# A transformer layer over 128 graphs: the MLP's first product as a 2x2 block product with seven block products

## The reference

```python
nx = _layernorm(x, ln1_g, ln1_b)
q, k, v = (nx @ W + b for Wq, Wk, Wv)           # 8 heads of 64
scores = jnp.where(adj_mask, q @ k.T / 8, NEG)
out = softmax(scores) @ v
x = x + out @ Wo + bo
nx = _layernorm(x, ln2_g, ln2_b)
return x + gelu(nx @ W1 + b1) @ W2 + b2         # W1: 512 x 2048, W2: 2048 x 512
```

## Time and profile before

| | |
|---|---|
| median of 3 runs | 2245.79 us (2245.63 to 2247.95) |
| profiled execution | 2246.27 us, span 2244.5 us |
| mean granted TensorE clock | 0.997 |
| TensorE busy | 2214.6 us, 13616 matmuls |
| VectorE busy | 1158.0 us |
| ScalarE busy | 720.1 us |
| GpSimd busy | 284.0 us |
| moved by DMA | 100.12 MB, mean 45 GB/s |

### The profile page before, as it was taken

How to read it: one execution, slowest core, us unless ns; L and a number is a source line. 1 busy time by engine, 2 the same in 40 slices (tenths; PEclk the granted TensorE clock), 3 DMA queues, 4 the chain that set the end, 5 groups by cost and what they waited for, 6 DMA issues and landing times.

```text
span 2244.5 us, 33957 instructions
## 1 busy us (share of the span) xinstructions
PE 2214.6 (99%) x13616; PEld 1827.9 (81%) x13616; DVE 1158.0 (52%) x1747; ACT 720.1 (32%) x1046; POOL 284.0 (13%) x217
## 2 busy tenths in 40 slices
PE   7999999999999989999999999999999999999999
PEld 6888888888888868888888888888888888888887
DVE  4887877777877764433434434434334334334321
ACT  4434333443333434322222222222223223223222
POOL 2121111111121124311011010010010110110100
PEclk9999999999999999999999999999999999999999
DMA  4221111211211133101101001001011011011000
GB/s 148 72 66 58 58 58 62 72 58 65 86 61 39 39 104 127 66 1 38 39 1 38 25 14 38 11 28 38 1 39 38 1 39 38 1 39 38 1 19 20
DMA packets 67363, 100.12 MB, mean 45 GB/s; under 512 B 17680, under 2 KB 21776, under 8 KB 67216
## 3 DMA queue, kind: packets, MB, share of 16 engines
q1 hardware_dynamic: 61696, 97.27, 13.0%
q10 hardware_dynamic: 5520, 0.55, 0.2%
HBM read 64.25 MB, written 33.55 MB: 44 GB/s over the span
## 4 chain that ended last, share of the span: by engine, by line
PE 96%; DVE 2%; ACT 1%; DMA 1%; POOL 0%; issue 0%; SPq 0%; DVEq 0%; ACTq 0%
PE lin L159 11%; PE ps_out L159 10%; PE ps_out L160 10%; PE ps_out L161 10%; PE ps_h L159 10%; PE ps_h L160 10%; PE ps_h L161 10%; PE lin L160 10%; PE lin L161 10%; PE ps_scores L1020 1%; PE lin L1047 1%; PE ps_probT L1030 1%; DMA raw<-in_L_gnn_W 0%; DMA x<-in_x 0%; POOL w_lo L464 0%
## 5 line engine op out<-in xcount | busy, mean ns | idle before, releaser
L902 DVE TENSOR_TENSOR hT_lo<-hT,hT_hi 128x512 fp32r<-128x512 f32 x256 | 181.4, 708 | 848.3 <-ACT hT_hi L639 848.3
L629 ACT ACTIVATE hT<-ps_h,b_cols 128x512 f32<-128x512 f32 x256 | 176.8, 691 | 976.0 <-PE ps_h L161 976.0
L159 PE MATMUL ps_h<-mlp_nxT_hi,w_lo 128*128 128x512 f32 x1024 | 399.9, 391 | 3.3 <-DVE mlp_nxT_lo L895 3.2
L161 PE MATMUL ps_h<-mlp_nxT_hi,w_hi 128*128 128x512 f32 x1024 | 399.1, 390 | 0.0
L160 PE MATMUL ps_h<-mlp_nxT_lo,w_hi 128*128 128x512 f32 x1024 | 399.1, 390 | 0.0
L159 PE MATMUL ps_out<-w_hi,hT_lo 128*128 128x512 f32 x1024 | 398.4, 389 | 0.6 <-POOL w_lo L464 0.6
L161 PE MATMUL ps_out<-w_hi,hT_hi 128*128 128x512 f32 x1024 | 398.3, 389 | 0.0
L160 PE MATMUL ps_out<-w_lo,hT_hi 128*128 128x512 f32 x1024 | 398.3, 389 | 0.0
L159 PEld LDWEIGHTS ps_h<-mlp_nxT_hi,w_lo 128*128 128x128 f32 x1024 | 192.5, 188 | 45.6 <-issue 3.7
L159 PEld LDWEIGHTS ps_out<-w_hi,hT_lo 128*128 128x128 f32 x1024 | 192.3, 188 | 41.0 <-issue 1.0
L161 PEld LDWEIGHTS ps_h<-mlp_nxT_hi,w_hi 128*128 128x128 f32 x1024 | 192.8, 188 | 40.0
(11 more groups left out here) (87 smaller groups left out, 2973.7 us busy)
## 6 DMA issues: line engine op xcount, KB each, us to landing
xres<-in_x SPq DMA_DIRECT2D x64, 256.0 KB, 3.0
x_scratch<-xres SPq DMA_DIRECT2D x64, 256.0 KB, 2.3
x<-x_scratch SPq DMA_DIRECT2D x16, 1024.0 KB, 5.6
out<-x SPq DMA_DIRECT2D x64, 256.0 KB, 2.5
x<-in_x SPq DMA_DIRECT2D x15, 1024.0 KB, 6.0
raw<-in_L_gnn_W SPq DMA_DIRECT2D x16, 512.0 KB, 3.4
x<-in_x SPq DMA_DIRECT2D x4, 256.0 KB, 4.4
qT<-in_L_gnn_Wq SPq DMA_DIRECT2D x1, 1024.0 KB, 8.2
```

Of the source, the lines that this page charges most:

```text
L159: pe.matmul(out, lhs[1], rhs[0], start=first, stop=False)
L161: return pe.matmul(out, lhs[0], rhs[0], start=False, stop=last)
L629: act.activation(hT[:, m % 2], ps_h[m % 2][:, :], ACT.Gelu, bias=b1_cols[:, m:m + 1]).then_inc(gelu_done, 1)
L902: dve.tensor_tensor(hT_lo[:, m % HR], hT[:, m % 2], hT_hi[:, m % HR].bitcast(F32), ALU.subtract).then_inc(h_split, 1)
```

## The change

Two groups of 512 tokens make a super-group (8 in all), the columns b1 and b2 of the right side. The 512 input channels are two halves of 256, and the 2048 hidden channels are taken as pairs of blocks, q and q + 8. So one step (64 in all: 8 super-groups x 8 values of q) is a 2x2 block product, a block being 128 hidden channels x 256 input channels times 256 x 512 tokens. It is made of seven block products of sums of blocks in place of eight. The results are C11 and C21 (first group), C12 and C22 (second). Products 1, 6, 7 and 4 add up in one bank, `ps_x`; ScalarE copies its state after 1, 6 and 7 (`snap`), and VectorE adds these copies to `ps_y` or `ps_z` (`add`) for C11, C12 and C22. C21 is what stands in `ps_x` after product 4. `down` of a step runs in the next step, between the products (`STEP`): tiles 0 to 3 into `ps_out` as before, tiles 4 to 7 into one bank `ps_r`, which VectorE adds into an SBUF tile `acc` after each (`add_acc`).

```diff
-LAST_ORDER = [("S", 0), ("L", 2), ("S", 1), ("L", 5), ("L", 8), ("P", 0), ("L", 11), ("O", 0), ("W", 0), ("P", 1),
-              ("W", 1), ("M", 0), ("M", 1), ("O", 1), ("M", 2), ("M", 3), ("F", 0), ("W", 2), ("W", 3)]
+LAST_ORDER = [("S", 0), ("L", 2), ("S", 1), ("L", 5), ("L", 8), ("P", 0), ("L", 11), ("O", 0), ("P", 1), ("F", 1),
+              ("W", 0), ("F", 5), ("W", 1), ("O", 1), ("F", 6), ("F", 2), ("W", 2), ("F", 7), ("W", 3)]
...
+SG = NG // 2
+NQ = FC // 2
+NSTEP = SG * NQ
+PROD = 7
...
+CONV = [1, 2, 5, 6, 7, 4, 3]
+BLOCKS = ["C11", "C22", "C21", "C12"]
+SNAPS = {"C11": 0, "C12": 1, "C22": 2}
+SNAP_OF = [1, 6, 7]
+STEP = [("P", 1), ("d", 0), ("P", 2), ("d", 4), ("P", 6), ("d", 1), ("P", 5), ("d", 5), ("P", 7), ("d", 2), ("d", 6),
+        ("P", 4), ("d", 3), ("P", 3), ("d", 7)]
+PREP = NQ
+def ln_tiles(g):
+    return [g - PREP] if PREP <= g < NG - 2 else [6, 7] if g == NG - 2 else []
```

```diff
+            def load_w1_job(q):
+                wait(sp, stage_stored, 64 * q)
+                for b, (m, c) in enumerate(((q + NQ, 0), (q, 0), (q, 2), (q + NQ, 2))):
+                    sp.dma_start(stage[:, b].rearrange("p (c n) -> p c n", n=P),
+                                 w1_cols[:, c:c + 2, m * P:(m + 1) * P]).then_inc(stage_loaded, 16)
+            def store_w1_job(q):
+                sp.wait_ge(stage_lo_done, 2 * q + 1)
+                for to, source in ((0, stage_hi.bitcast(F32)), (1, stage[:, 1:8])):
+                    sp.dma_start(w1_dram[q, :, to], source.rearrange("p b n -> p (b n)")).then_inc(stage_stored, 16)
+            def load_w2_job(q):
+                sp.wait_ge(stage_stored, 64 * q + 32)
+                sp.dma_start(stage[:, 0:4].rearrange("p (i b) n -> p i (b n)", i=2), w2_quads[q])\
+                  .then_inc(stage_loaded, 16)
+            def store_w2_job(q):
+                sp.wait_ge(stage_lo_done, 2 * q + 2)
+                for to, source in ((0, stage_hi[:, 0:4].bitcast(F32)), (1, stage[:, 0:4])):
+                    sp.dma_start(w2_dram[q, :, to], source.rearrange("p b n -> p (b n)")).then_inc(stage_stored, 16)
...
             def body(g, par):
-                if not isinstance(g, int) or g + 3 < NG:
+                if g + 3 < NG:
                     load_x(g + 3, 1 - par)
+                if g < PREP:
+                    load_w1_job(g)
                 if "U" in kinds_of(g):
                     load_mask(g + 1, 1 - par)
                 load_xres(g, 0)
                 load_xres(g, 1)
+                for n in ln_tiles(g):
+                    load_ln_tile(n)
                 if is_last(g):
...
+                if g < PREP:
+                    store_w1_job(g)
+                    load_w2_job(g)
                 store_x1(g, 0)
                 load_xres(g, 2)
                 store_x1(g, 1)
                 load_xres(g, 3)
...
                 store_x1(g, 2)
                 store_x1(g, 3)
...
+                if g < PREP:
+                    store_w2_job(g)
```

```diff
+            def job_sums(q):
+                pool.wait_ge(stage_loaded, 80 * q + 64)
+                a21, a11, a12, a22, s1, s2, s3, s4 = (stage[:, b] for b in range(8))
+                pool.tensor_tensor(s1, a21, a22, ALU.add).then_inc(stage_summed, 1)
+                pool.tensor_tensor(s3, a11, a21, ALU.subtract).then_inc(stage_summed, 1)
+                pool.wait_ge(stage_summed, 4 * q + 1)
+                pool.tensor_tensor(s2, s1, a11, ALU.subtract).then_inc(stage_summed, 1)
+                pool.wait_ge(stage_summed, 4 * q + 3)
+                pool.tensor_tensor(s4, a12, s2, ALU.subtract).then_inc(stage_summed, 1)
+            def job_lo(q, which):
+                pool.wait_ge(stage_hi_done, 2 * q + which)
+                part, hi = (stage[:, 1:8], stage_hi[:, :]) if which == 1 else (stage[:, 0:4], stage_hi[:, 0:4])
+                pool.tensor_tensor(part.bitcast(F32R), part, hi.bitcast(F32), ALU.subtract).then_inc(stage_lo_done, 1)
...
                 fill_neg(g, 0)
+                if g < PREP:
+                    job_sums(g)
                 bias_xres(g, 0)
                 bias_xres(g, 1)
                 fill_neg(g, 1)
                 if "N" in kinds_of(g):
                     rstd_of(g + 2)
...
+                for n in ln_tiles(g):
+                    ln_tile_rstd(n)
+                if g < PREP:
+                    job_lo(g, 1)
                 bias_xres(g, 2)
                 bias_xres(g, 3)
...
+                if g < PREP:
+                    job_lo(g, 2)
+                if g == NG - 2:
+                    t_sums(0)
+                    for n in range(4):
+                        t_sum(0, n)
+            def last_body(g):
+                fill_neg(g, 0)
+                conv_lo(0)
+                conv_lo(2)
+                fill_neg(g, 1)
+                conv_lo(3)
```

```diff
                 att_hi(g, 0)
                 unit(6)
+                if g < PREP:
+                    job_hi(g, 1)
                 exponent(g, 1)
                 unit(7)
                 take_probT(g, 1)
                 unit(9)
                 att_hi(g, 1)
                 unit(10)
+                if g < PREP:
+                    job_hi(g, 2)
...
+                for n in ln_tiles(g):
+                    ln_tile_affine(n)
+            def job_hi(q, which):
+                if which == 1:
+                    act.wait_ge(stage_summed, 4 * q + 4)
+                    act.activation(stage_hi[:, :], stage[:, 1:8], ACT.Copy).then_inc(stage_hi_done, 1)
+                else:
+                    act.wait_ge(stage_loaded, 80 * q + 80)
+                    act.activation(stage_hi[:, 0:4], stage[:, 0:4], ACT.Copy).then_inc(stage_hi_done, 1)
```

```diff
+            def load_w1(n):
...
+                else:
+                    sp.wait_ge(p_done[3], n - 1)
+                sp.dma_start(w1_ring[:, n % 2].bitcast(F32).rearrange("p s b n -> p s (b n)"), w1_dram[n % NQ])\
+                  .then_inc(w1_loaded[n % 2], 16)
...
+            def mlp_step(n):
+                s, q = n // NQ, n % NQ
+                if 1 <= n < NSTEP - 1:
+                    load_w1(n + 1)
+                if 2 <= n < NSTEP:
+                    load_w2(n)
+                if q == 0 and s > 0:
+                    for t in range(TILES):
+                        sp.wait_ge(out_done, TILES * (s - 1) + t + 1)
+                        sp.dma_start(out_tiles[2 * TILES * (s - 1) + t], xb[:, t, :]).then_inc(xb_stored, 16)
+                        sp.wait_ge(acc_added, TILES * (n - 1) + t + 1)
+                        sp.dma_start(out_tiles[2 * TILES * (s - 1) + TILES + t], acc(t)).then_inc(acc_stored[t], 16)
+                        if t > 0 and s < SG:
+                            load_acc(s, t - 1)
+                    if s < SG:
+                        load_acc(s, TILES - 1)
+                if q == 1:
+                    if s == 0:
+                        sp.wait_ge(u_done, UNITS * NG)
+                    wait(sp, xb_stored, 64 * s)
+                    load_xb(2 * (s + 1) if s < SG - 1 else 2 * s)
+                if q == 4 and s < SG - 1:
+                    sp.wait_ge(m_t_done, 2 * s + 1)
+                    load_xb(2 * (s + 1) + 1)
+                if q == 7 and s < SG - 1:
+                    sp.wait_ge(m_t_done, 2 * s + 2)
+                    load_xb(2 * s)
```

```diff
                 normalise(g, 1)
                 if ln:
                     ln_transpose(g + 2, par, 3, 6)
+                for n in ln_tiles(g)[:1]:
+                    ln_tile_norm(n)
+                for n in ln_tiles(g)[1:]:
+                    ln_tile_transposes(n - 1)
+                    ln_tile_var(n)
                 unit_v(2)
                 residual(g, 0)
...
                 if ln:
                     for k in range(KC):
                         nx_lo(g + 2, k)
+                for n in ln_tiles(g)[1:]:
+                    ln_tile_norm(n)
+                for n in ln_tiles(g)[-1:]:
+                    ln_tile_transposes(n)
                 residual(g, 2)
                 residual(g, 3)
...
+            def t_sum(s, n):
+                b11, b21, b12, b22 = (nx_from[i] for i in (1, 2, 7, 3))
+                t1, t2, t4 = (nx_from[i] for i in (5, 6, 4))
+                out, a, b = ((t1, b12, b11), (t2, b22, t1), (b12, b22, b12), (t4, b21, t2))[n]
+                wait(pool, t_summed, 4 * s + n)
+                pool.tensor_tensor(out, a, b, ALU.subtract).then_inc(t_summed, 1)
...
+            def mlp_super(s):
                 for t in range(TILES):
-                    bias_x1(g, par, t)
+                    bias_acc(s, t)
+                if s < SG - 1:
+                    m_rstd(2 * s)
+                    m_rstd(2 * s + 1)
+                    t_sums(s + 1)
+                    for n in range(3):
+                        t_sum(s + 1, n)
+                bias_xb(s, 0)
+                bias_xb(s, 1)
+                if s < SG - 1:
+                    t_sum(s + 1, 3)
+                bias_xb(s, 2)
+                bias_xb(s, 3)
```

(111 more changed lines are left out.)

646 lines of the change are left out of this document (341 added, 305 removed).

## The result

| | before | after |
|---|---|---|
| median of 5 runs (range) | 2245.69 us (2245.2 to 2247.95) | 2256.84 us (2254.59 to 2261.01) |
| ratio | | 1.0051, 95% interval 1.0037 to 1.0066 |
| span of the profiled execution | 2244.5 us | 2255.0 us |
| matmuls | 13616 | 13216 |

The forecast was 2216.7 us, range 2168 to 2248, with 0.11 for slower. It was wrong, and the time lies outside the range.

What follows compares the result with a forecast made beforehand. TensorE, busy 99% of the span, was taken as the bound. 2245.8 - 87.0 + 31.5 (preparation) + 8.4 (LN tiles) + 12 (borders) + 6 (seam) = 2216.7 us; stated range 2168 to 2248.

Steps and rivals of the forecast that it cites:

- Removed products: MLP stage: 384 fewer matmuls at a pitch of 0.2267 us, saving 87.0 us.
- Ordinary steps and the stream: MLP steps: VectorE, ScalarE and weight loads fit within 20.4 us a step, so nothing was charged.
- rival B: MLP steady step becomes bound by its chain, not TensorE: slower, 63 us per us a step; chance 0.09.
- The preparation: Weight sums in attention groups 0 to 7: 4.5 us for each of groups 1 to 7, 31.5 us, bounds 0 and 45.
- my three cases: TensorE's wait at W0 in a preparation group: 0 if loads land early, 3.2, or 6.4 us with the subtract blocked.
- The borders: Seven super-group borders: GpSimd's long sums hold VectorE, 1.7 us each, 12 us in all, bounds 3 and 25.
- the places that I named: At borders: add_acc 2 just in time for d7, C21's split late for d0, add_acc 1 about 1 us late for d6.
- LN tiles: Attention groups 8 to 13: 16 short VectorE transposes delay P0 by 1.4 us a group, 8.4 us, bounds 0 and 15.
- The seam: Attention to MLP: late fill delays group 15's first softmax 10.4 us; net cost 6 us, bounds -6 and +12.
- Rival C: Attention stalls of 6.4 us or more a group and borders at their upper bound: 2243 to 2256; chance 0.08.
- Rival A: Preparation hidden in attention, with loads landing by +9: near 2160, 2150 to 2180; chance 0.20.

Runs made afterwards that it cites:

- e10: Changed kernel with e4, e6, e7, seam fill first and small transposes spread, plus next group's fill earlier, W2 loads later and rounded last; 2155.25 us.
- e2: Changed kernel with GpSimd's subtracts in the preparation cut into pieces of 256 columns, order unchanged; 2239.56 us.
- e7: Changed kernel with GpSimd's border sums in pieces of 256 columns and biases of xb in halves, order unchanged; 2234.74 us.
- e4: Changed kernel with conv_lo 2 put behind C21's split and the C12 add on VectorE in a super-group's last step; 2241.37 us.
- e6: Changed kernel with e1 and e2, and the store of W2's sums put behind the next group's loads; 2212.2 us.
- e1: Changed kernel with w1 loads behind the mask and xres loads on SyncE, and the four sums behind rstd on GpSimd; 2239.15 us.

## Why the prediction was wrong

- **Removed products, -87.0**: right. The count fell by 400 (384 and 16 at the seam, as said), and the pitch stayed.
- **Ordinary steps and the stream, nothing**: right, 100.00 busy of 100.00 us; rival B did not come.
- **The preparation, +31.5: the step that failed.** Its parts came out nearly to the tenth: `rstd` at +19.4 (I had +19.6), the sums 0.73 us each, `att_lo(0)` over at +32.3 (+32.7), `W0` 6.2 us late (6.4). That is the worst of my three cases, with the subtract held until GpSimd's ends. I then took 4.5 us a group, a mean of cases that my own queue count had already told apart; the queue as I had traced it gave 6.4. And to that I added nothing for the clock. I charged the half clock behind a stall only at the seam, though the earlier trace rows had shown it behind 4.18 us; it came in each of the 7 groups, for about 1.7 us. Measured 7.6 a group (4.3 idle for `attT_lo`, 1.3 for `v`, most of the rest the half clock), 53.5 in all, beyond my upper bound of 45. This term alone moves the sum by 22.0, more than half of the 40.1 by which the forecast was off.
- **The borders, +12**: of the places that I named only `d0` came, behind C21's split, held as said; `add_acc` kept TensorE nowhere. The mechanism was right and the size wrong: 2.2 us idle at each of seven borders and 1.7 of half clock behind six, 25.5 us, at my upper bound of 25. The half clock was missing here too.
- **LN tiles, +8.4**: right, 8.2; 16 short transposes took 5.04 us. But I stopped at group 13. Body 13's block runs into group 14, where one unit fewer stands before `P0`: a wait of 4.08 us, half clock behind it, and 7.2 us in all, charged at nothing.
- **The seam, +6**: VectorE's mask waited 9.90 us for the fill and began 9.4 us later in its group than before (10.4 forecast), and the scores waited 7.96. Yet the seam and all else that is left come to 2.4 us. This is a remainder of the account and no measurement of the seam, so that the term came out near is not shown.
- **Rival C** (the stalls take it all, 2243 to 2256) is what happened, a little beyond its end. I gave it 0.08, because it needs several terms at their upper ends. The two large ones, preparation and borders, were not independent: one hold of VectorE, for a whole GpSimd instruction, and one clock penalty stood in both.
- **Rival A** (hidden) did not come in the kernel as it was written. It was a matter of order and of the length of GpSimd's instructions: e10, which changes both, has it, at 2155, with 2150 to 2180 forecast for it.

The Trainium skill (SBUF — State Buffer, section Who interferes with whom) has it that a VectorE instruction with two SBUF inputs contends with a GpSimd one that reads SBUF, and that the one that comes second is fully blocked. The runs agree for the whole of one GpSimd instruction (4.33 us against 1.22), and e2 and e7 show that VectorE is let in between two.

What stays open: pieces shorter than 256 columns were not tried, the half clock was not measured apart from the stalls that bring it, and no run tells why it stays away behind the first border.

## What to carry to other kernels

Where the queues place a two-input VectorE instruction beside a long GpSimd one, charge it until the GpSimd instruction ends and its own time after that, not a share; better, cut the GpSimd work into pieces of 256 columns and put it behind what VectorE's chain waits for. A load that is moved up a queue must be followed past every wait in that queue, the last body's stores too. Price a TensorE stall by its idle time and by the half clock behind it (1.7 us here, behind most stalls of 2.2 us and more), each time that it comes; and when several terms rest on one mechanism, their upper ends come together.

## What the runs showed of the hardware

- The length of an idle time of TensorE does not settle what follows it. Behind idle times of 5.06 us (group 4) and of 2.2 us (six borders) the granted clock was 0.50 for about 3.4 us, a matmul took 0.427 us, and about 1.7 us were lost. Behind the first border's 2.19 us it stayed at 1.00. An idle time of 2.49 us for `attT_lo` in group 14 was followed by 1.00 before (at 797.46) and by 0.50 after (at 865.59). Those of 1.03 us (e4), 1.43 us and 2.03 us (e6) were followed by 1.00, one of 1.83 us in e2 (at 242.34) by 0.50. I had expected only the long ones to cost it.
- An fp32 `tensor_scalar` of VectorE with one SBUF tensor input is slowed too: four normalisations took 3.60 us beside GpSimd's sums in e1 (at 288.53), 1.92 with GpSimd idle in the changed kernel (at 299.30). The sums were slowed as well, from 0.73 us to as much as 0.92.
